# A head's instructions in another order on TensorE, ScalarE and VectorE, and seven of eight second-pass masks as two GpSimd fills

## What is computed

```python
scores = jnp.einsum('bhqd,bhkd->bhqk', q, k) * SCALE + rel * alibi_slopes
scores = jnp.where(causal_mask, -jnp.inf, scores)
attn = jnp.maximum(jax.nn.softmax(scores, axis=-1), 1e-10)
attended = jnp.einsum('bhqk,bhkd->bhqd', attn, v)          # then @ out_w.T + out_b
# experts: RMS norm, router, top 4 of 32 experts, at most 128 tokens each (CAP)
y = (silu(buf @ w_gate) * (buf @ w_up)) @ w_down            # each expert, gathered rows
sh = silu(x @ sw_gate) * (x @ sw_up) @ sw_down              # shared expert, FS = 704
out = x_layernormed + scatter_add(y * weight) + sigmoid(x @ w_shared_gate) * sh
```

## Time and profile before

| | before |
|---|---|
| median of 3 runs | 633.17 us (631.96 to 634.8) |
| the profiled execution | 632.87 us |
| its span, first to last instruction | 630.9 us |
| mean granted TensorE clock | 0.963 |
| PE busy, matmuls | 559.0 us, 89% |
| PE weight loads busy | 385.3 us, 61% |
| DVE busy | 489.6 us, 78% |
| ACT busy | 444.4 us, 70% |
| POOL busy | 263.1 us, 42% |
| DMA, mean over the span | 113 GB/s |

### The profile page before, as it was taken

One profiled execution on the slowest core, in us unless ns is written; L12 is line 12 of the kernel. 1 busy time (PEld: TensorE's weight loads), 2 busy tenths in 40 slices (PEclk: granted clock), 3 DMA queues, 4 the chain that ended last, 5 costly groups with the idle time before them and its releaser, 6 DMA issues.

```text
span 630.9 us, 16914 instructions
## 1 busy us (share of the span) xinstructions
PE 559.0 (89%) x4584; PEld 385.3 (61%) x4584; DVE 489.6 (78%) x1098; ACT 444.4 (70%) x1021; POOL 263.1 (42%) x632
## 2 busy tenths in 40 slices
PE   1599559688999999999999999999999999999984
PEld 1594227455666666666666666666666666666763
DVE  5997964578778878887887788778878887887456
ACT  2322564268788878888888788888878888888670
POOL 7630000325444355445544554454355445544303
PEclk9959869799999999999999999999999999999997
DMA  8992255533335334434443353335334434532247
GB/s 251 178 241 80 101 175 200 162 88 61 97 86 116 90 95 104 104 92 103 95 115 85 85 111 95 86 87 119 89 92 101 104 100 120 126 96 55 58 149 137
DMA packets 74320, 71.44 MB, mean 113 GB/s; under 512 B 12786, under 2 KB 64692, under 8 KB 74164
## 3 DMA queue, kind: packets, MB, share of 16 engines
q1 hardware_dynamic: 65076, 59.28, 33.0%
q0 software_dynamic: 9136, 11.80, 12.3%
q10 hardware_dynamic: 80, 0.03, 0.0%
HBM read 47.82 MB, written 23.59 MB: 113 GB/s over the span
## 4 chain that ended last, share of the span: by engine, by line
PE 53%; ACT 16%; issue 11%; DVE 10%; DMA 6%; SPq 3%; ACTq 1%; DVEq 0%; POOLq 0%; POOL 0%
ACT PSB L1073 9%; PE PSB L908 7%; PE PSB L776 6%; PE PSB L802 6%; ACT PB L1082 6%; PE PSB L900 5%; PE PSB L824 5%; PE PSB L821 4%; PE PSB L879 4%; PE PSB L798 3%; PE PSB L772 2%; PE PSB L677 2%; DVE WDS L1288 2%; PE PSB L861 2%; DMA XN<-in_L_attn_qkv_dram 1%
## 5 line engine op out<-in xcount | busy, mean ns | idle before, releaser
L1353 DVE TENSOR_REDUCE NEGM<-PSB 128x1 f32<-128x1024 f32 (+7 forms) x256 | 192.3, 751 | 56.9 <-PE PSB L776 54.7
L1073 ACT ACTIVATE PSB<-PSB,NEGM 128x1024 f32<-128x1024 f32 (+7 forms) x256 | 182.5, 713 | 38.7 <-DVE NEGM L1353 38.5
L1082 ACT ACTIVATE PB<-PSB 128x128 f32<-128x128 f32 (+7 forms) x256 | 166.3, 651 | 32.3 <-PE PSB L802 30.7
L1359 DVE TENSOR_SCALAR PB<-PB 128x128 f32<-128x128 f32 (+7 forms) x256 | 117.3, 468 | 26.7 <-ACT PB L1082 24.4
L776 PE MATMUL PSB<-STACKS 111*128 111x512 bf16 (+3 forms) x384 | 105.5, 330 | 0.0
L802 PE MATMUL PSB<-STACKS 111*128 111x512 bf16 (+3 forms) x384 | 104.1, 326 | 0.0
L798 PE MATMUL PSB<-MK,IDB 128*128 128x128 bf16 x256 | 57.2, 224 | 17.5 <-ACT PSB L1073 13.7
L1671 POOL DMA_INDIRECT moe_rows<-YE,IDX x32 | 57.9, 1809 | 29.2 <-issue 29.2
L821 PE MATMUL PSB<-PB,VH 128*32 128x256 f32 x640 | 67.7, 384 | 0.0
L772 PE MATMUL PSB<-MQ,IDB 128*128 128x128 bf16 x256 | 58.1, 227 | 1.0 <-ACT UL L1060 0.5
L824 PE MATMUL PSB<-PB,VH 128*32 128x128 f32 x1024 | 55.5, 276 | 2.4 <-DVE PB L1359 2.4
(11 more groups left out here) (200 smaller groups left out, 1163.9 us busy)
## 6 DMA issues: line engine op xcount, KB each, us to landing
WGU<-in_L_ffn_w_gate_dram SPq DMA_DIRECT2D x32, 176.0 KB
WGU<-in_L_ffn_w_up_dram SPq DMA_DIRECT2D x32, 176.0 KB
WDS<-in_L_ffn_w_down_dram SPq DMA_DIRECT2D x32, 176.0 KB
q_parts<-PB SPq DMA_DIRECT2D x8, 384.0 KB, 2.6
STACKS<-q_parts SPq DMA_DIRECT2D x32, 96.0 KB
STACKS<-k_parts SPq DMA_DIRECT2D x32, 96.0 KB
XN<-in_L_attn_qkv_dram SPq DMA_DIRECT2D x4, 512.0 KB, 5.6
moe_rows<-XN SPq DMA_DIRECT2D x1, 2048.0 KB, 9.0
```

The source lines that it names most:

```text
L1073: act.activation(sc, sc, ACT.Exp, bias=NEGM[:, par, i:i + 1], accum_out=LSUM[:, par, i:i + 1]).then_inc(exp1_done, 1)
L1082: act.activation(PB[:, k % 2, prob_offset(s):prob_offset(s) + (s + 1) * P], psf[:, base:base + (s + 1) * P], ACT.Exp).then_inc(exp2_done, 1)
L1353: dve.tensor_reduce(NEGM[:, par, i:i + 1], psf[:, base:base + (i + 1) * P], AX_X, ALU.max, negate=True).then_inc(max_ready, 1)
L1359: dve.tensor_scalar(p, p, FLOOR, 0.0, ALU.subtract, ALU.max).then_inc(clamp_done, 1)
```

## The change

Masks: pass2(s) has its mask matmul only at s = 7; the others start with the score matmul. What is above the diagonal in the tiles s = 0 to 6 is set to zero in PB, after the clamp, by two affine selects on POOL for each head (`fill_diagonal`): part 0 over the diagonal blocks of the tiles 0 to 3 (128 x 4 x 128), part 1 over those of 4 to 6 (128 x 3 x 128). For one instruction to reach its blocks at one stride, `prob_offset` places the tiles in PB anew. Batch 0 of the value matmuls waits for the two fills (`fill_done`), batch 1 for the last clamp.

Order: the phases of PE, ACT and DVE are written out, with `first(s)` the first pass's part and `second(s)` the second's. `turn_rows` is ACT's now. `exp_seed` stands directly behind exp2(0). On POOL the gather precedes `prepare_values`, and the fills stand at the end of a phase, with `copy_scales`, `add_shared` and `copy_block` between them.

The diff, cut to its core; of the phases the new order alone:

```diff
 def prob_offset(s):
-    return s * (s + 1) // 2 * P
+    return 9 * P * s if s < NQ // 2 else P * (10 * (NQ - 1 - s) + 1)
+def diagonal(probs, tiles):
+    n = len(tiles)
+    if tiles.start < NQ // 2:
+        first, step, at = prob_offset(tiles.start), 9 * P, 0
+    else:
+        first, step, at = prob_offset(tiles[-1]) - 9 * P, 10 * P, 9 * P
+    return probs[:, first:first + step * n].rearrange("p (n c) -> p n c", c=step)[:, :, at:at + P]
+FILLED = (range(0, 4), range(4, 7))
 VALUE_BATCH = (range(0, 7), range(7, 8))
 LEAD = 2
...
                     pe.wait_ge(exp2_done, unit(it, k, NQ, s - 1))
                 w = P * (NQ - j)
                 key = KS[slot][0:ROWS, j * P:(j + 1) * P]
-                pe.matmul(psf[:, base:base + P], IDB[:, :], MK[:, :],
-                          start=True, stop=False, skip_group_check=True)
+                masked = s == NQ - 1
+                if masked:
+                    pe.matmul(psf[:, base:base + P], IDB[:, :], MK[:, :],
+                              start=True, stop=False, skip_group_check=True)
                 for c0 in reversed(range(0, w, 512)):
                     c1 = min(c0 + 512, w)
                     ins = pe.matmul(psf[:, base + c0:base + c1], key, QS[slot][0:ROWS, j * P + c0:j * P + c1],
-                                    start=(c0 > 0), stop=True, skip_group_check=True)
+                                    start=(c0 > 0 or not masked), stop=True, skip_group_check=True)
                 ins.then_inc(p2_ready, 1)
             def values(it, k, batch):
@@ -811,7 +825,10 @@
                     pe.wait_ge(o_evacuated, unit(it, k))
                     pe.wait_ge(v_ready, unit(it, k, 1, 1))
                     pe.wait_ge(c_turned, unit(it, k, 1, 2) if exists(it, k + 1) else UNITS)
-                pe.wait_ge(clamp_done, unit(it, k, NQ, VALUE_BATCH[batch][-1] + 1))
+                if batch == 0:
+                    pe.wait_ge(fill_done, unit(it, k, len(FILLED), len(FILLED)))
+                else:
+                    pe.wait_ge(clamp_done, unit(it, k, NQ, NQ))
                 for s, c in value_order(batch):
                     j, far = step_tile(s), NQ - 1 - c
                     probs = PB[:, par, prob_offset(s):prob_offset(s) + (s + 1) * P].rearrange("p (t q) -> p t q", q=P)
...
             def phase(it, k):
+                def second(s):
+                    if here:
+                        pass2(it, k, s, ahead)
+                first(0)
+                if turned:
+                    expert_down(it, w - 1, *aux_begin(it, w - 1, DN))
+                second(0)
+                first(1)
+                second(1)
+                if behind:
+                    values(it, k - 1, 0)
+                first(2)
+                second(2)
+                if behind:
+                    values(it, k - 1, 1)
+                first(3)
+                if block:
+                    expert_transpose(it, w, *aux_begin(it, w, TR))
+                second(3)
+                if block:
+                    shared(it, w, SA, 0)
+                if block:
+                    shared(it, w, SA, 1)
+                first(4)
+                second(4)
+                if exists(it, k + 1):
+                    c_transpose(it, k + 1)
+                first(5)
+                if block:
+                    expert_up(it, w, 0)
+                second(5)
+                if block:
+                    expert_up(it, w, 1)
+                first(6)
+                first(7)
+                second(6)
+                if block:
+                    shared(it, w, SB, 0)
+                if block:
+                    hidden_transpose(it, w)
+                if block:
+                    shared(it, w, SB, 1)
+                second(7)
...
+            def turn_rows(it, k):
+                o = aux_task(it, k, TR)
+                act.activation(XET[:, :, :].rearrange("p c m -> p (c m)"), o[:, 0:D], ACT.Copy).then_inc(xet_ready, 1)
...
+                    shared(it, w - 1, SB)
+                second(0)
+                if exists(it, k + 1):
+                    exp_seed(it, k + 1)
+                first(0)
+                second(1)
+                first(1)
+                second(2)
+                if turned:
+                    weigh(it, w - 1)
+                first(2)
+                second(3)
+                first(3)
+                if block:
+                    turn_rows(it, w)
+                if block:
+                    shared(it, w, SA)
+                second(4)
+                first(4)
+                second(5)
+                if block:
+                    tanh_gate(it, w, GU, CAP, F)
+                first(5)
+                second(6)
+                first(6)
+                first(7)
+                second(7)
...
+                    if here:
+                        clamp(it, k, s)
+                    if isinstance(it, int) and k == UNITS - 1 and s >= 2:
+                        if s == 3:
...
+                            gate((0, 0, 1, 2, 3)[s - 2])
+                first(0)
+                if behind:
+                    clamp(it, k - 1, NQ - 1)
+                first(1)
+                if turned:
+                    shared(it, w - 1, SB)
+                first(2)
+                first(3)
+                second(0)
+                second(1)
+                second(2)
+                if behind:
+                    evacuate_heads(it, k - 1)
+                first(4)
+                if exists(it, k + 1):
+                    turn_shift(it, k + 1)
+                second(3)
+                second(4)
+                first(5)
+                if block:
+                    shared(it, w, SA)
+                if block:
+                    gate_up(it, w)
+                first(6)
+                first(7)
+                if block:
+                    hidden_turned(it, w)
+                second(5)
+                second(6)
...
+            def fill_diagonal(it, k, part):
+                tiles = FILLED[part]
+                hold(pool, clamp_done, unit(it, k, NQ, tiles[-1] + 1))
+                d = diagonal(PB[:, k % 2, :], tiles)
+                pool.affine_select(out=d, in_=d, compare_op=ALU.is_ge, fill=0.0, base=0,
+                                   pattern=[[0, len(tiles)], [1, P]], channel_multiplier=-1).then_inc(fill_done, 1)
             def chain(it, k):
@@ -1687,10 +1784,12 @@
                     chain(it, k + 1)
                 if exists(it, w - 1):
                     scatter(it, w - 1)
+                if exists(it, w + 1):
+                    gather(it, w + 1)
                 if exists(it, k + 1):
                     prepare_values(it, k + 1)
-                if exists(it, w + 1):
-                    gather(it, w + 1)
+                if exists(it, k):
+                    fill_diagonal(it, k, 0)
                 if exists(it, w) and w % SLOTS == 0:
                     copy_scales(it, w)
                     if w >= SLOTS:
@@ -1700,6 +1799,8 @@
                     b, before = aux(it, w - 1, SB)
                     hold(pool, aux_ready[b], before + 1)
                     copy_block(it, w + 1)
+                if exists(it, k):
+                    fill_diagonal(it, k, 1)
```

93 lines of the change are left out of this document (24 added, 69 removed).

## The result

| | before | after |
|---|---|---|
| median | 632.57 us (631.61 to 634.8) | **609.71 us** (607.45 to 611.66) |
| ratio, 95% interval | | 0.9633 [0.9588, 0.9677] |
| profiled execution, its span | 632.87, 630.9 us | 607.45, 605.6 us |
| PE, DVE, ACT, POOL busy, us | 559.0, 489.6, 444.4, 263.1 | 546.3, 474.2, 451.7, 307.6 |
| mean granted clock | 0.963 | 0.956 |

The account below looks back on a forecast made before the run. PE bounds one head in four; in the others PE, DVE and ACT wait for each other. Short heads of 13.5 and long of 15.4 us save 25.9 us, masks at the end 0.4: 632.87 - 26.3 = 606.5 us, range 592 to 628.

Parts of the forecast that it names:

- (b): New order: down projection behind P1(0), silu behind M(1); exp1(1) 1.1 us sooner, 0.8 us of PE holes gone a head.
- The walk: The new order stepped through one short head with the old trace's durations, giving 13.2 us instead of 14.39.
- R3: Rival for the loop: masks lie in holes, the order frees no engine; 2 us gained, 631 us; chance 0.07.
- R1: Rival: order brings less; holes only move (first form, 621 us) or 2.4 us fills bind POOL (second, 617 us); chance 0.26.
- The sum: Four heads 3 x 13.5 + 15.4 = 55.9 us; 25.9 saved over 31 intervals, 0.4 at the end: 606.5 us.
- for what the walk holds at nothing: 0.3 us a head added to the walk's 13.2 for signals between engines, LEX and ports, making 13.5.
- The long head: One head in four, its shared-expert blocks down projections, bound by PE; its 16.13 us were to become 15.4.
- less 0.3 of its 0.5 us of holes: In the long head, the new order takes 0.3 of PE's 0.5 us of holes, besides 0.39 for masks.
- (a): Seven of eight second-pass mask matmuls removed from PE: 0.39 us a head, bounds 0 and 1.1.
- (c): Copy moved from DVE to ACT, covered by ACT's idle time; without that cover 0.47 us a head.
- (d): Two POOL selects a head, 0.62 and 0.51 us, 1.5 with waits, covered by waiting; after add_shared 0.2 to 0.6 lost.
- R2: Rival: POOL becomes the bound, fills standing still beside DVE clamps; decides from 3.3 us a head, 645 us; chance 0.08.

Follow-up runs that it names:

- down_late: The changed kernel with TensorE's expert down projection moved from ahead of pass2(1) to behind it: 633.9 us, ratio 0.9995.
- silu_early: The changed kernel with VectorE's gate of the shared experts put back ahead of the last tile's clamp and M(1): 620.96 us, ratio 0.9762.
- order_masks: The changed kernel's new order with all eight second-pass masks kept and no fills, values waiting for clamps: 612.24 us, ratio 0.9664.
- no_fills: The changed kernel without the two fills a head, masks still absent, batch 0 waiting for clamps: 607.51 us, ratio 0.9567.
- seed_late: The changed kernel with exp_seed (the LEX copy) moved back behind weigh (YE) on ACT: 685.6 us, ratio 1.0803.
- fills_thrice: The changed kernel with each of the two fills run three times over, each waiting for the one before: 719.21 us, ratio 1.1355.
- after_late_sum: The changed kernel, fills in the last head too, with the last addition of moe_rows behind the last head's clamps: 605.49 us, ratio 0.9561.
- tail_late_sum: The changed kernel, its last head with masks and no fills, and the last addition of moe_rows behind that head's clamps: 603.93 us, ratio 0.9528.
- last_masked: The changed kernel with the last head alone going back to masks and without fills: 605.58 us, ratio 0.957.

## Why the prediction was right

*The order (b).* The walk held step by step. Put and measured, in us from the head's start: M(0) 0.70 and 0.69, exp1(0) 2.0 and 1.95, M(1) 2.55 and 2.43, exp1(1) 3.65 and 3.55, exp1(3) 6.8 and 6.85, pass2(5) 8.95 and 9.15, pass2(6) 10.4 and 10.54, pass2(7) 12.7 and 12.67, the next head 13.2 and 13.18. down_late and silu_early show that the two moves I rested it on are worth 3.4 and 1.7 us in four heads, against 2.85 for the order as a whole: they don't add, each is needed. order_masks answers R3 and the first form of R1: the holes did not only move. The second form of R1 wanted fills of 2.4 us a head with their waits; they last 1.16 and cost the loop nothing.

*The sum.* It did not use the walk's 13.2 us for a short head but 13.5; 13.23 were measured. The 0.3 us I had added "for what the walk holds at nothing" was not there: the rows of before already held the signals. The long head I put at 15.4, and it is 15.87. The term that failed is "less 0.3 of its 0.5 us of holes": the order alone made it 0.1 longer (order_masks), and 0.5 us between starts on a saturated PE was no idle time that another order gives back. The two errors partly cancel: 55.9 forecast for four heads, 55.56 measured. They cancel once more in the whole. The change saved 25.6 us from the first to the 30th value start, where 3.34 for four heads would have given 24.2 over these 29 intervals. The last two intervals and the end, for which the forecast held another 1.7 + 0.4, lost 0.9, and the first value matmul came 0.6 earlier: 25.3 of span, against 26.3 forecast. That the time came within 1 us for the profiled execution is partly luck.

*The masks (a)* were mis-sized in their part: 0.39 us a head holds in the long one (0.36), while in the short ones of the new order 0.12 to 0.18 remain: 6 us over the loop (0.83 x 7.25), not 12, and 2.5 in the medians, as the end piece came out 3.0 us longer than order_masks'. The order brought 2.85 x 7.25 = 21 us in the loop, where I had split 26 about evenly.

*turn_rows (c)* at nothing: right, on either engine.

*The fills (d).* 0.64 and 0.52 us against 0.62 and 0.51 forecast; the second done at t=1.1 (1.2 forecast), values at 2.2 (2.1), LEX at 1.85 (1.9); free in the loop, as no_fills shows. POOL waits for LEX 1.2 us in four heads, not 11.8, and ACT never waits for LNS; the 0.2 to 0.6 us that I expected of it behind add_shared did not show.

*R2.* Its mechanism exists: seed_late and fills_thrice bring POOL's loop to the front, and beyond 3.3 us of added POOL time a head (1.5 with about 3 more in fills_thrice) the kernel is slower, as its point of decision said, though by 85 us, where its arithmetic, (11.5 + 4.5 - 14.81) x 31, gives 37. What I had not seen is that the early LEX is what keeps it away. I had listed LEX at 1.9 as a step of the walk and never as the condition for the fills to be free.

## What to carry to other kernels

An engine's busy share doesn't tell how much work it can take: POOL, 61% busy, had room for the two fills and for almost nothing more, since it is a chain of small dependent steps inside a loop with other engines. Before giving it work on which another engine waits, follow the loop round once (fill, values, down projection, LEX, chain, gather, fill) and move what closes it. What work removed from an engine is worth depends on the order around it: the seven masks gave 0.36 us in the head where PE was saturated, 0.12 to 0.18 in the other heads of the same order, and up to 0.35 (with an earlier LEX) in short heads of the old order, holes and all. A walk of the new order with the durations of the old trace was right to 0.2 us a step in the short heads, if nothing was added for safety.

## What was not expected of the hardware

- **A fill beside DVE operations can stand still for several of them in a row.** The select that takes 0.52 us alone took 2.62. When it began, DVE was in an operation of its own, and a clamp and two TENSOR_TENSORs followed without a gap; the select ended 0.38 us after the last of them. The earlier trace rows showed a step of POOL standing still for a clamp. It is not so each time: in after_late_sum the same select got in between two such operations (0.81 us), and the second of them took 1.00 us instead of 0.69. The Trainium skill, SBUF — State Buffer, Who interferes with whom, says that a tensor_scalar in a two-port mode, and a TENSOR_TENSOR with both inputs in SBUF beside a GpSimd instruction that reads SBUF, contend with GpSimd. The durations agree, though no row shows an operation's mode.
- **The cost of an affine select** is 0.64 us at 512 elements a partition and 0.52 at 384, with 0.29 at 128.
- **A short stand of PE costs twice.** After 6.1 us without matmuls the clock of the next 5.4 us was 0.54, mostly the 1.2 GHz level, and the value matmuls of the last head took 4.0 us (588.64 to 592.63), against 2.3 in tail_late_sum at a clock of 1.00 (588.17 to 590.45).
- **The prologue varies by more than the loop.** With the same instructions up to there, the first value matmul started between 155.7 and 161.5 us in four profiled executions (the changed kernel, last_masked, after_late_sum, tail_late_sum), while most heads repeated to 0.02 us. What sets it was not tried. For changes of 1% the distance of the heads tells more than the total.
